# A graph-attention kernel: the destination term of the first layer's scores moved from a TensorE product to ScalarE's bias

## What is computed

```python
xl = (x @ W).reshape(B, N, H, F)
asrc = jnp.einsum('bnhf,hf->bnh', xl, a_src)
adst = jnp.einsum('bnhf,hf->bnh', xl, a_dst)
e = jax.nn.leaky_relu(asrc[:, :, None, :] + adst[:, None, :, :], NEG_SLOPE)
e = jnp.where(mask[..., None], e, NEG_INF)
attn = jax.nn.softmax(e, axis=1)
out = jnp.einsum('bsdh,bshf->bdhf', attn, xl)
```

## Time and profile before

| | us |
|---|---|
| median of 3 runs | 763.97 (763.64 to 764.99) |
| the profiled execution, its own time | 768.98 |
| its span | 767.1 |
| PE busy | 716.1 |
| DVE busy | 684.1 |
| ACT busy | 592.6 |
| POOL busy | 536.5 |

### The profile page before, as it was taken

One profiled execution on the slowest core, in us unless ns is written; L12 is line 12 of the kernel. 1 busy time (PEld: TensorE's weight loads), 2 busy tenths in 40 slices (PEclk: granted clock), 3 DMA queues, 4 the chain that ended last, 5 costly groups with the idle time before them and its releaser, 6 DMA issues.

```text
span 767.1 us, 26536 instructions
## 1 busy us (share of the span) xinstructions
PE 716.1 (93%) x8398; PEld 592.9 (77%) x8398; DVE 684.1 (89%) x2017; ACT 592.6 (77%) x1865; POOL 536.5 (70%) x733
## 2 busy tenths in 40 slices
PE   0689999999999999999999999999999999999973
PEld 0477788888878888888888888888887888888852
DVE  5878999999999999999999999999998999999772
ACT  0368888888877888887888888878887788788852
POOL 6558777777667677767777777677776767776651
PEclk9999999999999999999999999999999999999996
DMA  7123466756666565676566566665575556555574
GB/s 198 41 53 67 99 114 112 112 122 122 109 111 113 117 116 115 114 121 113 112 118 119 115 115 115 109 119 112 125 116 103 113 108 115 116 119 98 86 117 96
DMA packets 270423, 84.70 MB, mean 110 GB/s; under 512 B 242896, under 2 KB 269904, under 8 KB 270288
## 3 DMA queue, kind: packets, MB, share of 16 engines
q1 hardware_dynamic: 269856, 82.24, 58.1%
q10 hardware_dynamic: 432, 0.79, 0.5%
HBM read 15.86 MB, written 8.39 MB: 32 GB/s over the span
## 4 chain that ended last, share of the span: by engine, by line
PE 65%; DVE 13%; DMA 7%; issue 6%; SPq 4%; ACT 4%; POOL 1%; DVEq 0%; POOLq 0%; ACTq 0%
PE bank L928 24%; PE bank L954 8%; PE bank L1104 6%; PE bank L1064 5%; DMA hT<-h_split 5%; PE bank L1083 3%; PE bank L1045 3%; PE bank L1053 3%; PE bank L980 3%; DVE top L848 2%; SPq L297 2%; SPq L273 2%; ACT e L554 2%; PE bank L1006 1%; PE bank L1004 1%
## 5 line engine op out<-in xcount | busy, mean ns | idle before, releaser
L554 ACT ACTIVATE e<-bank,nmx,q_power 128x128 f32<-128x128 f32 x512 | 194.6, 480 | 5.1 <-DVE nmx L853 4.9
L408 POOL CAST e_split<-e 128x512 f16<-128x512 f32 x128 | 89.7, 701 | 116.7 <-ACT e L554 116.7
L410 POOL TENSOR_TENSOR e_split<-e,e_split 128x512 f16<-128x512 f32 x128 | 152.2, 1189 | 10.3
L954 PE MATMUL bank<-w,h1T 128*128 128x258 f32 x512 | 122.6, 381 | 0.0
L422 POOL TENSOR_TENSOR rstd<-var,minus_half 128x1 f32<-128x1 f32 x128 | 71.7, 560 | 66.4 <-DVE var L718 66.4
L928 PE MATMUL bank<-w_split,hT 128*128 128x260 f16 x768 | 98.2, 278 | 11.6 <-DMA hT<-h_split 6.3
L954 PEld LDWEIGHTS bank<-w,h1T 128*128 128x128 f32 x512 | 96.5, 190 | 15.7 <-DVE h1T L749 1.6
L505 ACT ACTIVATE eT<-lr,nmx 128x128 f32<-128x128 f32 x256 | 102.6, 456 | 0.8 <-DVE nmx L805 0.8
L928 PE MATMUL bank<-h2T,proj_split 128*128 128x128 f16 x1536 | 96.2, 219 | 1.5 <-DMA h2T<-h_split 1.5
L928 PEld LDWEIGHTS bank<-h2T,proj_split 128*128 128x128 f16 x1536 | 90.8, 98 | 3.7 <-DMA h2T<-h_split 2.1
L928 PEld LDWEIGHTS bank<-w_split,hT 128*128 128x128 f16 x768 | 71.1, 98 | 23.7 <-DMA hT<-h_split 8.3
(11 more groups left out here) (120 smaller groups left out, 1905.6 us busy)
## 6 DMA issues: line engine op xcount, KB each, us to landing
x_in<-in_x_dram SPq DMA_DIRECT2D x64, 128.0 KB, 2.4
out_dram<-x_out SPq DMA_DIRECT2D x64, 128.0 KB, 2.0
adj_in<-in_adj_dram SPq DMA_DIRECT2D x64, 64.0 KB, 2.4
e3T<-e_split SPq DMA_TRANSPOSE x128, 3.1
hT<-h_split SPq DMA_TRANSPOSE x64, 2.4
h2T<-h_split SPq DMA_TRANSPOSE x64, 2.5
attT<-att_split SPq DMA_TRANSPOSE x64, 2.7
w<-in_L_gnn_W_dram SPq DMA_DIRECT2D x2, 256.0 KB, 6.1
```

The source lines that it names most:

```text
L408: pool.tensor_copy(e3_split[:, g.two, half, 0], e).then_inc(s[high_set], 1)
L410: pool.tensor_tensor(e3_split[:, g.two, half, 1], e, e3_split[:, g.two, half, 0], ALU.subtract).then_inc(s[low_set], 1)
L554: ins = act.activation(e3[:, g.two, h, :], S[:, h // 4, (h % 4) * N:(h % 4 + 1) * N], ACT.Exp, bias=nmx3[:, g.two, h:h + 1], scale=q_power ...
L954: ins = pe.matmul(X2[:, 0:D + 2], h1T[:, g.two, k * F:(k + 1) * F], w2[:, k, :], start=k == 0, stop=k == H - 1)
```

## The change

The destination term is no longer added by PE. DVE copies the four destination columns out of the bank as `a_dst`, times the same power of two, in `ab_low` ahead of the instruction that was there; ACT's leaky relu takes it as its per-partition bias. Since the bias differs by head, the one activation over 512 columns becomes four over 128. The table `pick` loses its half for the destination term.

```diff
-        pick = sb("pick", [128, 2, H, 128], F16)
+        pick = sb("pick", [128, H, 128], F16)
+        a_dst = sb("a_dst", [128, 2, H])
...
             def gat1_leaky(g):
...
-                act.activation(lr[:, g.two, :], Z[:, :], ACT.Prelu, scale=power[:, 1:2], alpha=SLOPE).then_inc(s["lr_set"], 1)
+                done(act, s["dst_set"], g)
+                for h in range(H):
+                    ins = act.activation(lr[:, g.two, h * N:(h + 1) * N], Z[:, h * N:(h + 1) * N], ACT.Prelu, bias=a_dst[:, g.two, h:h + 1],
+                                         scale=power[:, 1:2], alpha=SLOPE)
+                ins.then_inc(s["lr_set"], 1)
...
             def ab_low(g):
+                free(dve, s["lr_set"], g)
+                dve.tensor_scalar(a_dst[:, g.two, :].rearrange("p (a c) -> p a c", a=2), XL[:, :, HF // 2 + 2:HALF], power[:, 1:2], None,
+                                  ALU.mult).then_inc(s["dst_set"], 1)
                 done(dve, s["ab_high"], g)
...
             def scores1(g):
...
-                pe.matmul(Z[:, :], abT[:, g.two, :], pick[:, 1].rearrange("p h m -> p (h m)"), start=False, stop=False)
                 for h in range(H):
-                    ins = pe.matmul(Z[:, h * N:(h + 1) * N], pick[:, 0, h, :], abT[:, g.two, :], start=False, stop=h == H - 1)
+                    ins = pe.matmul(Z[:, h * N:(h + 1) * N], pick[:, h, :], abT[:, g.two, :], start=False, stop=h == H - 1)
```

More of the change, by code:

```diff
@@ L205, in gnn_kernel @@
             stats2_set mv2_set var2_set rstd2_set z2_set
-            hT_high hT_set xl_done xl_set ab_zero ab_high ab_set abt_done abT_set zsc_done lr_set nmx_set eT_set rs_set eTn_set
+            hT_high hT_set xl_done xl_set ab_zero ab_high ab_set dst_set abt_done abT_set zsc_done lr_set nmx_set eT_set rs_set eTn_set
             zmask_done et_done en_set o1_done ex_set h1T_set x2_done xl2_set ab2_set diag2_set zsc2_done lr2_set
@@ L344, in picks @@
             def picks(g):
-                pool.memset(pick[:, :, :, :], 0.0).then_inc(s["pick_set"], 1)
-                for n in range(4):
-                    side, row = pick[:, n % 2].rearrange("p (a c) m -> p a c m", a=2), 2 * H * (n // 2) + 2 * (n % 2)
+                pool.memset(pick[:, :, :], 0.0).then_inc(s["pick_set"], 1)
+                for n in range(2):
+                    side, row = pick.rearrange("p (a c) m -> p a c m", a=2), 2 * H * n
                     pool.wait_ge(s["pick_set"], n + 1)
@@ L1001, in scores1 @@
                 if g.n == 0:
-                    pe.wait_ge(s["pick_set"], 5)
+                    pe.wait_ge(s["pick_set"], 3)
                 done(pe, s["abT_set"], g)
-                pe.matmul(Z[:, :], abT[:, g.two, :], pick[:, 1].rearrange("p h m -> p (h m)"), start=False, stop=False)
                 for h in range(H):
-                    ins = pe.matmul(Z[:, h * N:(h + 1) * N], pick[:, 0, h, :], abT[:, g.two, :], start=False, stop=h == H - 1)
+                    ins = pe.matmul(Z[:, h * N:(h + 1) * N], pick[:, h, :], abT[:, g.two, :], start=False, stop=h == H - 1)
                 ins.then_inc(s["zsc_done"], 1)
```

## The result

The changed kernel takes 811.42 us (median of five, 810.92 to 812.51) against 763.97 us (median of five too, 761.96 to 765.78): ratio 1.061, 95% interval 1.059 to 1.063, so 47.4 us slower. It lies in the range, 9 us above the forecast of 802. Its profiled execution took 812.0 us with a span of 810.2.

What follows compares the result with a forecast made beforehand. PE's queue and a ring through ACT and the elu were taken as equally long, 10.88 us; 0.62 (ACT) + 0.10 (DVE) a step over 60 steps is 43 us, less 5 is 38: 802 us, range 782 to 823.

Steps and rivals of the forecast that it cites:

- The two loops of one length: PE's own work and a ring project2, turned heads, five ACT pieces, elu, project2 both take 10.88 us a step.
- The rival in which PE decides alone: The ring has hidden slack, 0.94 us needed, so PE's saved product counts: 764 - 14 = 750 us; chance 0.07.
- the ring over the elu: From project2 through PE to the turned heads, five ACT pieces and the elu, back to project2; grows 0.72 us a step.
- ACT's part: Four leaky relus for one in ACT's queue: 1.30 us instead of 0.68, so the ring grows 0.62 us a step.
- the deduction of 20 ns for each activation: Leaky relu taken as shorter than exponential L554, as over 512 columns (677 against 702 ns): four cost 1.38 - 0.08 = 1.30 us.
- the estimate of 1.54 us from the Trainium skill's figures: Four leaky relus at 386 ns each by the skill's page, about 817 us in sum; set aside for the trace rows.
- DVE's part: a_dst ahead of the split columns that PE's transpose awaits: 0.14 us of queue, 0.10 a step left on the ring.
- The 0.04 us thought to be free for it: Gap between DVE's split columns ending and PE's transpose load starting, 0.04 us free after some 0.05 for a semaphore.
- The prediction's own sign for a dearer a_dst: If PE waits for the split columns by more than 0.2 us, a_dst was dearer than taken.
- The places of PE's waits: PE caught first at aggregate2 by some 0.5 to 0.6 us, the rest at project2; idle about 0.9 us a step.
- The cushion: PE's 6.3 us of waits for late transposed inputs of project1 gain slack; 5 us taken back.
- The rival of the pushed exponentials: Delayed multi-head exponentials, split by POOL and turned by DMA for mha_av, make a second ring: 826 us or more; chance 0.05.

Runs made afterwards that it cites:

- the cure for that one: The kernel with both moves, with POOL's first split of the exponentials put last in its list and SP's list reordered to fit: 787.67 us, ratio 1.030.
- the kernel with both moves: Changed kernel with a_dst behind the low split columns, elu_exp, gat2_copy and elu moved ahead, gat1_recip moved behind att_norm: 810.56 us, ratio 1.059.

## Why the prediction was right, and where it was off

**The two loops of one length** held. The product's removal alone gained 1.3 us of the 14 that PE's queue would have given, within what can be measured. The rival in which PE decides alone needed 0.94 us of slack and had next to none. The sum was drawn up for the ring over the elu, though, and the chain of the changed kernel lies on the other one. Both contain the leaky relus and a_dst, so the number hardly depends on which of them holds; in this the forecast was lucky.

**ACT's part** was named rightly and sized too low. The step that failed is the deduction of 20 ns for each activation: over 512 columns the leaky relu is shorter than the exponential, over 128 columns with two pointers it is not, start to start. Four took 1.37 us, against 1.38 for the exponentials and 1.30 in the sum. The ring grew by 0.69 and not 0.62, which is 4 us of the 9 that were missing. The row nearest in form, unreduced, would have been right; the estimate of 1.54 us from the Trainium skill's figures was too high by 0.17, the sum's value too low by 0.07.

**DVE's part.** a_dst costs its queue 0.13 us (0.14 was taken). The 0.04 us thought to be free for it was there only while ACT had one activation: the run with one leaky relu shows 0.10 a step, as in the sum, but the changed kernel is 0.84 - 0.69 = 0.15 above the old step. The difference of 0.05 us a step is 3 us. The prediction's own sign for a dearer a_dst, a wait of more than 0.2 us for the split columns, came: 8.5 / 32 = 0.27 us. The chain shows why it is not free: it lies with the four activations on the ring over `gat1_exp`. The prediction had said of this ring only that it sets DVE's place in the step; with a_dst moved it is still the longer of the two, by the 0.10 us that moving the reciprocal gained.

**The places of PE's waits** were half wrong. Aggregate2 was expected to catch PE first; it was `project_v`, by the bank shared with the scores, a wait that the sum did not know. In the changed kernel it cost nothing, as its move showed: in a ring one wait takes the place of another. The waits at the three places come to 0.97 us a step, as long as the 0.9 expected; PE's busy share is 90% and not 87%, since its busy time does not fall with its work.

**The cushion.** The late transposes behind PE's waits for project1 went, as expected, from the 6.3 us of the earlier trace rows to 0.7:

```profile
PE bank L935 <- DMA hT<-h_split: 0.7, 1, 0.7
```

For the profiled executions the sum closes to 2 us: 60 x 0.84 = 50, less 5.6, is 45, and 812.0 - 769.0 = 43. The medians lie 47.4 apart. The profiled execution of before was 5.0 us above its median, so a part of its 6.3 us of waits is probably not in the median run; the 5 us taken back was then too much by two or three. This is argued and not shown, since there is only one trace of that kernel.

**The rival of the pushed exponentials** did not occur in the changed kernel, whose POOL has more room than before. It occurred as soon as the exponentials were put behind the elu. It began as the rival had said, at POOL's split of them, but went on through the second norm's power behind it in POOL's queue, and not through the DMA for mha_av.

## What to carry to other kernels

Work that is taken from the busiest engine is worth nothing if a ring through other engines is as long as its queue. The sign here was the busiest engine's starting right behind a result from another: 0.05 us between the elu and the weight load. A broadcast term as ScalarE's bias cost ScalarE's queue nothing while one bias served the whole instruction (0.66 us to the next start against 0.67); split in four it cost 0.69 us a step, for a product of 0.22, and half of that was the second pointer. In such a schedule a small instruction is priced by its place, 7.5 us for 0.13 us of queue, and a list should not be reordered before the pieces behind each moved one have been followed on every engine: the reordering made to save time made a third ring, and after the cure for that one DVE had hardly any idle time left.

## What the runs showed of the hardware

DVE instructions of one shape took two to four times as long where a certain POOL instruction ran beside them. The fourfold case is L860 above, 0.90 against 0.23 us. In the kernel with both moves the normalisation of x_in and the split of h have only one DVE instruction between them (L787, not shown); POOL begins its multiplication L400 while the first runs (timeline, 409 to 412 us):

```profile
410.23 0.45 DVE L728 SCALAR_TENSOR_TENSOR z<-x_in,mv,rstd 128x256 f32<-128x256 f32 x1
410.39 1.19 POOL L400 TENSOR_TENSOR eTn<-eT,rs 128x512 f32<-128x512 f32 x1 [1.02 <-DVE rs L851]
...
410.93 0.93 DVE L701 SCALAR_TENSOR_TENSOR h_split<-z,h_split 128x256 f16<-128x256 f32 x1
```

In the kernel after, where POOL's multiplication has begun before L728, that one takes 0.93 us and the L701 behind it 0.49. No run was made for it alone, so that the neighbour is the cause is read from these coincidences, and it may depend on which of the two starts first: L728, which here started before POOL's, was not held up.
